# Cross-attention on one core: order of a step's transfers, late value tails, and the place of the bias addition

## The reference

```python
q = _split_heads(hidden_states @ w_q, HEADS)
k, v = _split_heads(text @ w_k, HEADS), _split_heads(text @ w_v, HEADS)
out_text = _merge_heads(_sdpa(q, k, v))
k_ip, v_ip = _split_heads(ip_h @ w_k_ip, HEADS), _split_heads(ip_h @ w_v_ip, HEADS)
out_ip = _merge_heads(_sdpa(q, k_ip, v_ip, mask=mask_ip))
out = (out_text + IP_SCALE * out_ip) @ w_out + b_out
out = out + residual
```

## Time and profile before

| | us |
|---|---|
| median of three runs | 1266.85 |
| lowest and highest of these runs | 1266.1 and 1272.72 |
| span of the profiled execution | 1263.2 |
| TensorE busy in it | 1158.1 (92%) |
| GpSimd busy in it | 904.7 (72%) |
| VectorE busy in it | 1044.3 (83%) |

### The profile page before, as it was taken

The page is one execution under the profiler, slowest core; times in us unless marked ns, Lnnn a source line. Parts: engine busy times, 40 slices in busy tenths (PEclk is TensorE's granted clock), DMA queues, the critical chain, the costliest instruction groups (busy, mean ns, idle before and its releaser), DMA issues.

```text
span 1263.2 us, 34240 instructions
## 1 busy us (share of the span) xinstructions
PE 1158.1 (92%) x12734; PEld 1114.9 (88%) x12734; DVE 1044.3 (83%) x2054; ACT 897.6 (71%) x1923; POOL 904.7 (72%) x1004
## 2 busy tenths in 40 slices
PE   6998887559999999999999999999999999999996
PEld 5898787459999999999999999999999999999985
DVE  5687975669888889888898888888888888898972
ACT  2343343448888888877888888888888888887773
POOL 0111101038889889988988988898898899898896
PEclk9999999779999999999999999999999999999998
DMA  6388887645555545544455554454555555555431
GB/s 173 66 181 168 156 182 149 102 91 111 116 116 120 120 114 121 120 115 114 114 120 120 121 117 115 115 116 115 117 117 115 118 120 117 123 117 114 102 82 61
DMA packets 361460, 151.31 MB, mean 120 GB/s; under 512 B 298640, under 2 KB 350864, under 8 KB 360016
## 3 DMA queue, kind: packets, MB, share of 16 engines
q1 hardware_dynamic: 361296, 149.13, 52.9%
HBM read 88.17 MB, written 39.90 MB: 101 GB/s over the span
## 4 chain that ended last, share of the span: by engine, by line
PE 53%; POOL 11%; DMA 11%; SPq 9%; DVE 6%; issue 5%; ACT 2%; POOLq 0%; ACTq 0%; DVEq 0%
PE ps_a L832 9%; DMA q_hi_extra<-q_hi_lo 8%; PE ps_o L903 8%; PE ps_s L873 7%; PE ps_m L854 6%; PE ps_s L879 6%; PE ps_b L832 6%; POOL prob_lo L1402 6%; PE ps_k L199 2%; PE ps_v L199 2%; SPq L617 2%; SPq L668 2%; POOL y L1396 2%; DMA x_keep<-in_x_dram 2%; PE ps_a L918 2%
## 5 line engine op out<-in xcount | busy, mean ns | idle before, releaser
L1402 POOL TENSOR_TENSOR prob_lo<-prob,prob_hi 128x512 f16<-128x512 f32 (+1 forms) x448 | 506.1, 1148 | 106.0 <-ACT prob_hi L1071 106.0
L873 PE MATMUL ps_s<-q_hi_lo,keys 128*128 128x256 f32 x960 | 248.9, 299 | 44.3 <-DMA q_hi_extra<-q_hi_lo 42.9
L1070 ACT ACTIVATE prob<-ps_s 128x512 f32<-128x512 f32 (+1 forms) x448 | 254.2, 567 | 35.4 <-PE ps_s L879 31.0
L1071 ACT ACTIVATE prob_hi<-ps_s 128x512 f16<-128x512 f32 (+1 forms) x448 | 252.8, 564 | 0.0
L879 PE MATMUL ps_s<-q_hi_extra,keys 128*128 128x256 f32 x960 | 234.1, 281 | 0.3 <-ACT q_hi_extra L1058 0.3
L1298 DVE TENSOR_REDUCE stats<-ps_m 128x8 f32<-128x552 f32 x320 | 231.2, 722 | 0.0
L873 PEld LDWEIGHTS ps_s<-q_hi_lo,keys 128*128 128x128 f32 x960 | 172.6, 190 | 54.1 <-issue 37.4
L903 PE MATMUL ps_o<-values,prob_hi 128*128 128x68 f16 (+7 forms) x3584 | 200.9, 193 | 1.5 <-DVE heads L1312 1.5
L903 PE MATMUL ps_o<-values,prob_lo 128*128 128x68 f16 (+3 forms) x1792 | 190.8, 193 | 0.0
L903 PEld LDWEIGHTS ps_o<-values,prob_hi 128*128 128x128 f16 x3584 | 174.9, 98 | 13.0 <-issue 1.6
L879 PEld LDWEIGHTS ps_s<-q_hi_extra,keys 128*128 128x128 f32 x960 | 173.5, 190 | 0.5 <-ACT q_hi_extra L1058 0.5
(11 more groups left out here) (180 smaller groups left out, 2999.1 us busy)
## 6 DMA issues: line engine op xcount, KB each, us to landing
x_in<-in_x_dram SPq DMA_DIRECT2D x64, 320.0 KB, 3.8
q_hi_extra<-q_hi_lo SPq DMA_DIRECT2D x64, 320.0 KB, 3.4
x_keep<-in_x_dram SPq DMA_DIRECT2D x64, 320.0 KB, 3.2
out_dram<-y SPq DMA_DIRECT2D x128, 160.0 KB, 1.8
k_scratch<-k_stage SPq DMA_DIRECT2D x16, 770.0 KB, 5.8
keys<-k_scratch SPq DMA_DIRECT2D x256, 48.1 KB, 2.1
ctx_in<-in_ctx_dram SPq DMA_DIRECT2D x64, 128.0 KB, 2.8
keys<-k_scratch SPq DMA_DIRECT2D x256, 24.1 KB, 1.9
```

Source lines behind the costliest of these rows:

```text
L873: mm(ps, keys[:, n, 0, quad, c:c + P], q_hl[n][:, quad, :], start=i == 0, stop=False)
L1070: nc.scalar.activation(prob[:, s, 0:w], ps_s[(b[1] + s) % 2][:, 0:w], ACT.Exp)
L1071: nc.scalar.activation(prob_hi[par(b)][:, s, 0:w], ps_s[(b[1] + s) % 2][:, 0:w], ACT.Exp).then_inc(s_hi, 1)
L1402: nc.gpsimd.tensor_tensor(prob_lo[par(b)][:, s, 0:w], prob[:, s, 0:w], prob_hi[par(b)][:, s, 0:w], ALU.subtract).then_inc(s_lo, 1)
```

## The change

On SyncE a step's transfers stand in another order, and some belong to another batch than before: the copy of q stays first; then the store of batch n-3 (was n-2), the residual of n-1 (was n), the keys of n+2 (was n+3), the values of n+2, x of n+4, and one tile of the value tails in each of steps 1 to 7. The waits of `load_keys` and the rest follow the new batch numbers. The two stores of the last batch stand behind the loop. On GpSimd `add_bias()` moves from behind `rest(1)` to behind `add_heads(1)`. Nothing else is changed, and the instructions are the same in kind and number.

```diff
                     def step(sp, b, n):
-                        E, A, Bs, Cs, Ds = has(n)
-                        if A:
+                        if 0 <= n + 1 < NB:
                             copy_q(off(b, 1))
-                        if n is None or n + 4 < NB:
+                        if 0 <= n - 3 < NB:
+                            store(off(b, -3), 0)
+                            store(off(b, -3), 1)
+                        if 0 <= n - 1 < NB:
+                            load_residual(off(b, -1))
+                        if 3 <= n + 2 < NB:
+                            sp.wait_ge(s_sc, at(b, PAIRS, 0))
+                            load_keys(off(b, 2))
+                        if 2 <= n + 2 < NB:
+                            sp.wait_ge(s_vx, at(b, 3, 3))
+                            load_values(off(b, 2))
+                        if n + 4 < NB:
                             sp.wait_ge(s_xt, at(b, 1, 3))
                             load_x(off(b, 4))
-                        if Ds:
-                            store(off(b, -2), 0)
-                            store(off(b, -2), 1)
-                        if Bs:
-                            load_residual(b)
-                        if n is None or 0 <= n < NB - 2:
-                            sp.wait_ge(s_vx, at(b, 3, 3))
-                            load_values(off(b, 2))
-                        if n is None or 0 <= n < NB - 3:
-                            sp.wait_ge(s_sc, at(b, PAIRS, PAIRS))
-                            load_keys(off(b, 3))
-                        if n in (0, 1):
-                            for u in range(4 * n, min(4 * n + 4, len(TILES_IN))):
-                                store_tail(1, u)
+                        if 0 <= n - 1 < len(TILES_IN):
+                            store_tail(1, n - 1)
 
                     sched(sp, step)
+                    for t in range(NT):
+                        store((None, NB - 1, 1), t)
...
                             rest(0)
                             rest(1)
-                        if Cs:
-                            add_bias()
                         if Bs:
                             rest(2)
                             rest(3)
...
                         if Cs:
                             add_heads(1)
+                            add_bias()
                         if E:
                             place_mask(off(b, 2))
```

## The result

The changed kernel takes 1278.69 us, the median of 20 runs, beside 1267.11 us for the kernel before in as many: a ratio of 1.0087, 95% interval 1.0076 to 1.0097. It is slower by 11.6 us, and 1280.0 was forecast. The profiled execution has a span of 1273.6 us, 10.4 above that of before.

A forecast was written before the change was run, and what follows sets the result against it. TensorE's wait for the late copy of q was taken to bound the kernel. Its 0.65 us gain included, the step grows 0.22 us to 15.59, + 13 us over 60 steps: 1266.85 + 13 = 1280 us, range 1257 to 1291.

The forecast's parts named there:

- The copy of q: SyncE: the copy behind the stores makes TensorE's first scores wait; the new order removes this 0.65 us a step.
- The path behind N: GpSimd after the normalisation: the moved bias delays `rest(6)`, TensorE's unit 1 waits 0.87 us, step becomes 15.59 us.
- N: End of the second normalisation on VectorE in a step, the zero point for the times.
- The five terms: GpSimd: start 0.08, heads 1.10, bias 1.52, held mask 0.51, `rest(6)` 0.67, ending 3.88 us after the normalisation.
- The collision: VectorE's spread of values waits out GpSimd's bias, then holds the mask, which takes 0.51 us to the next start.
- The bound of 0.16: GpSimd's mask without being held: step 15.24 us, 1259 us in all; rival with chance 0.15.
- The mask's branch: VectorE's first maximum waits for the later mask: ring of 15.2 us, short of 15.59 by 0.4, not the bound.
- the copy isn't late: Judges the rival that SyncE's list still makes the copy late: no change, 1267 us, chance 0.1.
- VectorE lost no turn: Judges the rival that VectorE's spread often waits through several GpSimd instructions: 1300 us, chance 0.1.
- TensorE isn't held: Rival: `rest(6)` ends in time for TensorE's unit 1, if bias under 1.0: step 14.72, 1228 us, chance 0.05.
- Part 2: SyncE: 13 value-tail issues move from steps 0 and 1 to steps 1 to 7, hidden in idle time; zero effect.
- the ring of neither copy nor bias: Two loops: `finish`, stores, copy, scores; and normalisation, heads, bias, mask, `rest(6)`, sum of heads, 15.59 us a step.

The follow-up runs named there:

- bias_r2: Changed kernel with the bias addition behind `rest(2)` instead of behind `add_heads(1)`: 1225.88 us, ratio 0.9666 to the kernel before.
- half_bias: Changed kernel with the bias added to only one of the two row tiles: 1233.69 us, ratio 0.9739 to the kernel before.
- small_spread: Changed kernel with VectorE's first spread of values cut from 800 to 160 columns: 1258.96 us, ratio 0.9929 to the kernel before.
- bias_last: Changed kernel with the bias addition behind `rest(6)`, ahead of `finish`: 1244.52 us, ratio 0.9802 to the kernel before.
- mask_first: Changed kernel with the mask copy ahead of the bias addition: 1272.6 us, ratio 1.0033 to the kernel before.
- sp_only: Changed kernel with the bias addition back behind `rest(1)`, new SyncE order kept: 1251.84 us, ratio 0.9859 to the kernel before.
- bias_r3: Changed kernel with the bias addition behind `rest(3)`: 1242.9 us, ratio 0.9808 to the kernel before.
- bias_mid: Changed kernel with the bias addition behind `rest(4)`: 1277.16 us, ratio 1.0081 to the kernel before.
- tails_only: Kernel before with only the value tails moved, one tile in each of steps 1 to 7: 1271.98 us, ratio 1.0038.
- bias_only: Kernel before, old SyncE order, with only the bias addition moved behind `add_heads(1)`: 1321.05 us, ratio 1.0406.
- mid_old_sp: Kernel before, old SyncE order, with only the bias addition moved behind `rest(4)`: 1305.83 us, ratio 1.0301.

## Why the prediction was right, point by point

- **The copy of q.** Its wait is gone from the steady part, as said, and stays away in every kernel with the new order and comes back in each with the old one. The 0.65 us a step that it was said to cost, and the 14.72 without it, are confirmed by bias_r2's step of 14.71. Only the 9.9 us from stores to copy were those of a long step: over the 56 steps they lie between 7.6 and 10.1, mostly at about 8.4 where no issue is slow, and this one holds the slow issue of 1.59 us.
- **The path behind N.** The five terms were 0.08 + 1.10 + 1.52 + 0.51 + 0.67; the rows of after have 0.09, 1.11, 1.49, 0.50 and 0.67. Unit 1 starts at N + 3.92 (said 3.93), the next N is 11.63 behind (said 11.66), the step 15.55 (said 15.59). half_bias and small_spread shorten a term each, and the step shrinks by as much; bias_last takes the bias out and TensorE's wait there is gone.
- **The size.** The step grew by 0.20 from 15.36, where 0.22 from 15.37 was said; over 60 steps that is 12 in place of 13 us, and 11.6 were measured.
- **The collision.** The mask takes 0.55 in the median, as said, and the spread 1.79. The bound of 0.16 was rightly left: the turn of the two engines is the same in every step (the mask takes 0.54 to 0.56 in all).
- **The mask's branch.** It was said to be short of the bound by 0.4. VectorE waits 9.1 / 55 = 0.17 us a step for the mask, and it is indeed not the bound: with the mask early (mask_first) the step is shorter by 0.10 only. That it is worth nothing at all is not so.
- **The rivals.** TensorE is held, the copy isn't late, and no spread of after lasts more than 1.80: VectorE lost no turn. The point given for "TensorE isn't held", a bias under 1.0, was too generous: with 0.80 half_bias still waits 0.2 us a step, since the hold of the mask has to be counted too.
- **Part 2 and the residual.** "Zero" was right for this change, but only because the copy no longer stands behind the tails (5 us in the old order by the medians, 7 in the profiled execution, about half of them by the fallen clock) and because the bias leaves its old place (1.2 us of waiting a step for the residual, sp_only). Each was costed with the other parts in place, and neither of these prices was seen.

What the prediction didn't ask is how the whole came to + 11.6. Against bias_r2, which has the ring of neither copy nor bias, before is 41 us slower by the copy and after 53 by the bias. The change removes the one ring in full and puts in the other; that the two nearly cancel is no law, and another place of the bias would have turned the sign.

## What to carry to other kernels

When a wait on a transfer goes, measure the step that the compute engines would have without it (here 14.7), and follow every moved instruction to the next one that TensorE waits for, hold by the neighbour engine included. Put movable work on an in-order engine ahead of its idle gaps, not behind them, no earlier than its input lands: beyond the step of bias_r2, one and the same 1.5 us instruction cost 0.24, 0.31, 0.44, 0.81 or 0.85 us a step by its place alone (bias_r3, bias_last, sp_only, bias_mid, after). Parts of a reordering are not additive: the new order of transfers alone gave 17 us, the new place of the bias alone cost 53 us, and both together cost 12. Look at the granted clock of single steps when some are much longer than the others: a long wait can cost more than its own length.

## What the runs showed of the hardware

The hold between VectorE's spread and GpSimd has two sides. The spread of 800 columns waits for the GpSimd instruction in flight, so its length follows that one's (1.79 behind a bias of 1.55, 1.10 behind the half one of 0.87, 0.58 alone). GpSimd then loses 0.33 to 0.36 us, whatever it begins: mask 0.19 to 0.55, low part 0.67 to 1.00, the 128x64 part of the heads 0.32 to 0.66, bias 1.56 to 1.90. A spread of 160 columns costs it 0.02 (0.19 to 0.21). The Trainium skill, page SBUF — State Buffer, section SBUF: two separate sides, lets whichever starts first keep the pair of ports for the whole instruction. By it GpSimd should lose the 0.58 of a spread; the traces agree on who waits for whom, and the loss they show is 0.35.

The Trainium skill, page Perfetto Trace Analysis, section GPSIMD Engine Instruction, has GpSimd timed by start to start. The traces agree: after's bias is shown as 1.55 and takes 1.49 to the next start, and the prediction's step, a sum made of starts, was right to 0.04 us.

TensorE's granted clock fell to its lower level in single steps of the kernels in which it waited longest for the copy: two in tails_only, four in bias_only, one in mid_old_sp (18.86 us). Before each it stood idle for 1.7 to 2.9 us. Other waits of this length were followed by none, so the wait alone doesn't decide it, and what else does is open.

Unexplained is a slow issue on SyncE now and then: of the transfers of keys most take 0.43 us, but 29 of 448 take 0.95 to 1.89 in before between 325 and 1185 us, and 12 of 444 in after. In before this matters: 36 of the 56 stretches from stores to copy hold an issue of some transfer of over 0.9 us, they last 9.4 us in the mean where the others last 8.6, and they are followed by 20.5 of the 27.2 us that TensorE waits for the copy. The slow issues are thus a good part of what makes the copy late; no run takes them away. In the new order no wait of TensorE came from them.
